# One Trainium2 core, attention and a state-space scan: statistics of seven batches, the last chunk's gates, the rooms of the end and two pools of PSUM banks are placed anew

## What is computed

```python
x1 = x * s1[:, None, :]
x1 = (x1 - mu) * rsqrt(var + 1e-5)                  # per token
q, k = heads(x1 @ Wq.T * q_dc), heads(x1 @ Wk.T * k_dc)      # 16 heads of 32
v = x1 @ Wv.T * v_dc * s2
x = x + (softmax(q k' / sqrt(32)) v) @ Ww.T * w_dc + v @ Wu.T * u_dc
xr, gate = split(x @ W_in.T)                         # 1024 each
xn = layernorm(silu(conv4(xr + cond))) * ln_g + ln_b
B, C, dt = split(xn @ W_xproj.T);  dt = tanh(dt @ W_dt.T + b_dt) * 0.01
h = clip(h * (1 - dt * tanh(A_log)) + B * min(|xn|, 1) * xn_t, -10, 10)   # 1024 steps
x = x + ((C . h + D * xn) * silu(gate)) @ W_out.T
```

## Time and profile before

| what | us |
|---|---|
| median of 3 timed runs (7177.43 to 7194.07) | 7184.33 |
| profiled execution | 7179.22 |
| its span | 7177.1 |

### The profile page before, as it was taken

The page is one execution under the profiler, slowest core; times in us unless marked ns, Lnnn a source line. Parts: engine busy times, 40 slices in busy tenths (PEclk is TensorE's granted clock), DMA queues, the critical chain, the costliest instruction groups (busy, mean ns, idle before and its releaser), DMA issues. The chain is left out here.

```text
span 7177.1 us, 72778 instructions
## 1 busy us (share of the span) xinstructions
PE 6304.4 (88%) x24000; PEld 2629.8 (37%) x24000; DVE 4763.7 (66%) x5810; ACT 2326.0 (32%) x4453; POOL 3308.7 (46%) x2631
## 2 busy tenths in 40 slices
PE   3899989999998999999865889999999989999897
PEld 1344434444343444444332223333333333333223
DVE  4554554555454555555426988889898889889890
ACT  1243343433444343343423223223232323223101
POOL 4366465665656574565714233324234343324312
PEclk7799999999999999999977779899998989899999
DMA  5221222222222222212123233434334333334432
GB/s 159 53 86 54 79 65 84 79 62 85 54 79 74 79 73 62 84 51 85 38 95 93 74 86 107 110 84 112 90 106 110 106 110 101 108 81 113 107 90 81
DMA packets 416040, 618.30 MB, mean 86 GB/s; under 512 B 59152, under 2 KB 192528, under 8 KB 415152
## 3 DMA queue, kind: packets, MB, share of 16 engines
q1 hardware_dynamic: 378800, 563.28, 27.8%
q10 hardware_dynamic: 36864, 50.38, 2.8%
HBM read 310.36 MB, written 201.38 MB: 71 GB/s over the span
## 5 line engine op out<-in xcount | busy, mean ns | idle before, releaser
L1018 POOL TENSOR_TENSOR acc<-acc,prob 128x512 f32<-128x512 f32 x1536 | 1903.2, 1280 | 1190.3 <-PE bank L737 954.7
L946 DVE TENSOR_REDUCE mx<-bank 128x1 f32<-128x512 f32 x2048 | 1322.3, 686 | 785.6 <-PE bank L707 783.9
L1710 DVE SCALAR_TENSOR_TENSOR g<-xps,bd,g 128x1024 f32<-128x1024 f32 x1024 | 1313.4, 1283 | 220.7 <-PE xps L1498 145.2
L707 PE MATMUL bank<-khat,qhat 96*128 96x512 f32 x2048 | 1010.2, 531 | 39.0 <-DMA khat<-halves 16.5
L1716 DVE TENSOR_SCALAR g<-g,lim 128x1024 f32<-128x1024 f32 x1024 | 1007.9, 984 | 28.6
L858 ACT ACTIVATE prob<-misc 128x512 f32<-128x512 f32 x1195 | 682.7, 601 | 567.9 <-PE misc L724 382.3
L1498 PE MATMUL xps<-sx,spread 16*128 16x512 f32 x2048 | 539.4, 529 | 279.3 <-DVE g L1710 263.0
L1861 POOL TENSOR_TENSOR y_t<-y_t,dx_t 128x512 f32<-128x512 f32 x120 | 172.4, 1457 | 1286.9 <-DMA y_t<-scratch_y 1286.9
L1513 PE MATMUL yps<-g,cexp 128*32 128x512 f32 x4096 | 709.3, 688 | 11.3 <-DVE g L1716 11.2
L724 PE MATMUL misc<-qhat,khat 98*128 98x512 f32 x1366 | 596.2, 464 | 131.2 <-ACT prob L858 104.6
L707 PEld LDWEIGHTS bank<-khat,qhat 96*128 96x128 f32 x2048 | 379.9, 194 | 546.6 <-issue 371.5
(11 more groups left out here) (183 smaller groups left out, 7038.8 us busy)
## 6 DMA issues: line engine op xcount, KB each, us to landing
sx<-scratch_xhl SPq DMA_DIRECT2D x512, 128.0 KB, 4.9
scratch_dx<-dx SPq DMA_DIRECT2D x64, 512.0 KB, 3.9
scratch_xhl<-xhi SPq DMA_DIRECT2D x64, 512.0 KB, 5.2
scratch_xhl<-xn SPq DMA_DIRECT2D x64, 512.0 KB, 5.5
scratch_y<-ysb SPq DMA_DIRECT2D x512, 64.0 KB
dx_t<-scratch_dx SPq DMA_DIRECT2D x60, 512.0 KB, 6.1
y_t<-scratch_y SPq DMA_DIRECT2D x60, 512.0 KB, 3.5
qhat<-halves SPq DMA_DIRECT2D x384, 64.0 KB, 2.0
```

What stands on the lines that cost most here:

```text
L707: pe.matmul(bank[m][:, 0:QC], self.qhat[0:96, s, h, qt * P:(qt + 1) * P], self.khat[0:96, s, h, c * QC:(c + 1) * QC], start=True, stop=Tru ...
L946: dve.tensor_reduce(self.mx2[:, j // self.NQ, c:c + 1], bank[m][:, 0:QC], AX.X, ALU.max).then_inc(sem[f"dve_m{m}"], 1)
L1018: pool.tensor_tensor(self.acc[:, a, h, :], self.acc[:, a, h, :], self.prob[:, (n % 2) * GH + h, :], ALU.add).then_inc(sem["pool_acc"], 1)
L1710: dve.scalar_tensor_tensor(self.g[:, t % 4, :], self.xps[t % 2][:, :], self.bd[:, i % 2, tl:tl + 1], self.g[:, (t - 1) % 4, :], ALU.mult, ...
```

## The change

It has five parts.

- **Statistics.** The set-up takes the statistics of batch 0 alone. Its x is loaded ahead of the last three weights into `x0`, a view of `aoT`, multiplied there on GpSimd, and normalised from there. The other batches get a lane `statistics(b)` in the unit before (fractions 0.2 to 1.6 of the batch before's first unit): loads, GpSimd products, VectorE's mean and variance, one Sqrt on ScalarE, the reciprocal. The normalisation loads and multiplies these tiles again, as before.
- **Order of the start.** TensorE begins the plan after the last demodulation sums are read, ScalarE after batch 0's statistics; only the copies (`lay`) and GpSimd still wait for the stored rows. The first batch's values come behind its projection. The ones in khat are written by GpSimd.
- **Maxima by blocks.** The 64 tiles go in four blocks of query half and key half; a tile waits for its two of the four laid halves. The lanes of `project` and `maxima` get other fractions.
- **Pools.** Scores may take banks 0 to 3, side work banks 2 to 5.
- **End.** The last chunk's gates (`gates`: `zm` on TensorE, `zo` on ScalarE) run beside the last chunk's steps and go into `xn` and `xc`; `finish` of the last chunk has no gates of its own and three rooms, whose buffers are others than before.

```diff
+def score_tile(j, TT, NQ):
+    blocks = sorted(((qc, kc) for qc in range(NQ) for kc in range(NQ)), key=lambda v: (max(2 * v[0], 2 * v[1] + 1), v))
+    each = GH * TT // NQ
+    qc, kc = blocks[j // each]
+    h, t = divmod(j % each, TT // NQ)
+    return h, qc * (TT // NQ) + t, qc, kc
...
 def attention_plan(plan, B, TT, NQ):
     plan.bank = {}
     order = Order(plan, 8, (0.2, 0.5))
-    EXP, SIDE = (0, 1, 2), (3, 4, 5)
+    EXP, SIDE = (0, 1, 2, 3), (2, 3, 4, 5)
     U, n_steps = B * GROUPS, NQ * TT
     def lane():
         out = []
         return out, lambda *a, **k: out.append(item(*a, **k))
+    def statistics(b):
+        out, put = lane()
+        put("SP", 0.6, ("sb_row", b), (("nb_mul", b - 1, TT - 1),) if b > 1 else (), [("ld_brow", 16)], lands=3.0)
+        for tt in range(TT):
+            s = tt % 2
+            old = ("sb_st", b, tt - 2) if tt > 1 else ("nb_nrm", b - 1, TT - 2 + tt)
+            put("SP", 0.6, ("sb_ld", b, tt), (old,) if b > 1 or tt > 1 else (), [(f"ld_xn{s}", 16)], lands=3.0)
+            put("POOL", 1.3, ("sb_mul", b, tt), (("sb_row", b), ("sb_ld", b, tt)), [("pool_n", 1)])
+            put("DVE", 0.7, ("sb_st", b, tt), (("sb_mul", b, tt),), [("dve_st", 1)])
+            put("DVE", 0.2, ("sb_ag", b, tt), (("sb_st", b, tt),), [("dve_st", 1)])
+        put("DVE", 0.2, ("sb_e", b), (("sb_ag", b, TT - 1),), [("dve_st", 1)])
+        put("ACT", 2.9, ("sb_sq", b), (("sb_e", b),), [("act_sq", 1)])
+        put("DVE", 0.3, ("sb_r", b), (("sb_sq", b),), [("dve_st", 2)])
+        return out
     def normalise_batch(b):
         out, put = lane()
-        put("SP", 0.6, ("nb_row", b), (("nb_mul", b - 1, TT - 1),) if b else (), [("ld_brow", 16)], lands=3.0)
         for tt in range(TT):
             s = tt % 2
-            old = ("nb_nrm", b, tt - 2) if tt > 1 else ("nb_nrm", b - 1, TT - 2 + tt)
-            put("SP", 0.6, ("nb_ld", b, tt), (old,) if b or tt > 1 else (), [(f"ld_xn{s}", 16)], lands=3.0)
-            put("POOL", 1.3, ("nb_mul", b, tt), (("nb_row", b), ("nb_ld", b, tt)), [("pool_n", 1)])
+            if b:
+                old = ("nb_nrm", b, tt - 2) if tt > 1 else ("sb_st", b, TT - 2 + tt)
+                put("SP", 0.6, ("nb_ld", b, tt), (old,), [(f"ld_xn{s}", 16)], lands=3.0)
+                put("POOL", 1.3, ("nb_mul", b, tt), (("nb_ld", b, tt),), [("pool_n", 1)])
             old = ("nb_tr", b, tt - 1) if tt else ("nb_tr", b - 1, TT - 1)
-            put("ACT", 0.6, ("nb_nrm", b, tt), (("nb_mul", b, tt),) + ((old,) if b or tt else ()), [("act_n", 1)])
+            put("ACT", 0.8, ("nb_nrm", b, tt), (("nb_mul", b, tt), ("sb_r", b)) * (b > 0) + ((old,) if b or tt else ()),
+                [("act_n", 1)])
             g = ("nb_tr", b, tt)
...
         out, put = lane()
-        put("SP", 0.6, ("mv_row", b), (("mv_o", b - 1, TT - 1),) if b else (), [("ld_vrow", 16)], lands=3.0)
+        put("SP", 0.6, ("mv_row", b), (("mv_o", b - 1, TT - 1),) if b else (("nb_ev", 0, TT - 1),),
+            [("ld_vrow", 16)], lands=3.0)
+        first = () if b else (("pm", 0, 2 * NQ - 1, HT - 1),)
         used = tuple(("C", b * GROUPS - 2 - k, n_steps - 1) for k in range(3)) if b else ()
         used += (("sk_tr", b - 1, TT - 1),) if b else ()
         for tt in range(TT):
             g = ("mv", b, tt)
...
             g = ("mx", u, j)
-            put("PE", 0.24, g, tuple(("cat", u, k, part) for k in range(2 * NQ) for part in range(2)),
+            _, _, qc, kc = score_tile(j, TT, NQ)
+            put("PE", 0.24, g, tuple(("cat", u, k, part) for k in (2 * qc, 2 * kc + 1) for part in range(2)),
                 [("pe_m{m}", 1)], take=SIDE, group=g)
             put("DVE", 0.69, ("mr", u, j), (g,), [("dve_m{m}", 1)], group=g, give=True)
...
         if u + 1 < U:
-            side(project(u + 1), -0.2, 0.05)
-            side(maxima(u + 1), 0.1, 0.85)
+            side(project(u + 1), -0.1, 0.15)
+            side(maxima(u + 1), 0.05, 0.85)
         if g == 0:
             side(finish_batch(b - 1), 0.1, 0.7) if b else side(scale_weights(0, 1), 0.1, 0.9)
+        if g == 0 and b + 1 < B:
+            side(statistics(b + 1), 0.2, 1.6)
         if g == 1:
             side(skip_path(b), -0.1, 0.9)
...
         c, n = divmod(k, 2)
         s, to = u % 2, (self.qhat, self.khat)[n]
+        w.wait_ge(sem["st_rows"], 16)
         w.wait_ge(sem["act_hi"], plan.after("act_hi", ("hi", u, k)))
         self.of_bank(w, "dve", ("pm", u, k), ("lo", u, k))
...
         tiles = lambda a: a.rearrange("(t p) o -> p t o", p=P)
         sp.dma_start(self.condT[:, :, :], d["condT"].rearrange("(t p) b -> p t b", p=P)).then_inc(sem["ld_cond"], 16)
+        for n, name in enumerate(("wqT", "wkT")):
+            sp.dma_start(self.wsq[:, n, :, :], tiles(d[name])).then_inc(sem[f"ld_w{n}"], 16)
+        sp.dma_start(self.brow[:, 0, :], d["cond"][0, 0:HID].partition_broadcast(P)).then_inc(sem["ld_s1"], 16)
+        for n in range(self.TT // 2):
+            sp.dma_start(self.x0[:, 2 * n:2 * n + 2, :], tiles(d["x"][0, 2 * n * P:2 * (n + 1) * P, :])).then_inc(
+                sem[f"ld_x0{n}"], 16)
+        for n, name in enumerate(("wvT", "wwT", "wuT")):
+            sp.dma_start(self.wsq[:, 2 + n, :, :], tiles(d[name])).then_inc(sem[f"ld_w{2 + n}"], 16)
         sp.dma_start(self.s2row[:, :], d["cond"][:, HID:2 * HID]).then_inc(sem["ld_s2"], 16)
-        for n, name in enumerate(("wqT", "wkT", "wvT", "wwT", "wuT")):
-            sp.dma_start(self.wsq[:, n, :, :], tiles(d[name])).then_inc(sem[f"ld_w{n}"], 16)
         sp.dma_start(self.wv[:, :, :], tiles(d["wvT"])).then_inc(sem["ld_wv"], 16)
-        for b in range(self.B):
-            w.wait_ge(sem["s_pool"], (b - 1) * self.TT)
-            sp.dma_start(self.s1b[:, b % 2, :], d["cond"][b, 0:HID].partition_broadcast(P)).then_inc(
-                sem[f"ld_s1{b % 2}"], 16)
-            for tt in range(self.TT):
-                i = b * self.TT + tt
-                w.wait_ge(sem["s_pool"], i - 3)
-                sp.dma_start(self.xin[:, i % 4, :], d["x"][b, tt * P:(tt + 1) * P, :]).then_inc(
-                    sem[f"ld_xs{i % 4}"], 16)
-        w.wait_ge(sem["s_dve"], 6)
-        sp.dma_start(d["rows"], self.rows[:, :, :]).then_inc(sem["st_rows"], 16)
     def sync(self, sp):
         d, sem, plan, w, TT, QC = self.d, self.sem, self.plan, Waits(sp), self.TT, self.QC
-        w.wait_ge(sem["st_rows"], 16)
-        w.wait_ge(sem["x_dve"], 2 * self.B * self.TT + 4)
-        w.wait_ge(sem["s_act"], 10)
-        w.wait_ge(sem["s_pe"], 4)
         tiles = lambda a: a.rearrange("(t p) o -> p t o", p=P)
...
         sem, plan, w, TT, QC = self.sem, self.plan, Waits(pe), self.TT, self.QC
         ident, bank = self.ident, self.bank
-        w.wait_ge(sem["st_rows"], 16)
-        w.wait_ge(sem["ld_wv"], 16)
-        w.wait_ge(sem["x_dve"], 2 * self.B * TT + 4)
...
         w.wait_ge(sem["ld_cond"], 16)
         act.activation(self.condT[:, :, :], self.condT[:, :, :], ACT.Square).then_inc(sem["s_act"], 1)
-        for n in range(5):
+        for n in range(2):
+            w.wait_ge(sem[f"ld_w{n}"], 16)
+            act.activation(self.wsq[:, n, :, :], self.wsq[:, n, :, :], ACT.Square).then_inc(sem["s_act"], 1)
+        w.wait_ge(sem["x_dve"], 2 * self.TT + 1)
+        act.activation(self.rstd[:, 0:self.TT], self.rstd[:, 0:self.TT], ACT.Sqrt).then_inc(sem["x_act"], 1)
+        for n in range(2, 5):
             w.wait_ge(sem[f"ld_w{n}"], 16)
             act.activation(self.wsq[:, n, :, :], self.wsq[:, n, :, :], ACT.Square).then_inc(sem["s_act"], 1)
...
+LAST_ROOMS = 3
+def room_before(i, b, room, NCH, B):
+    step = LAST_ROOMS if i == NCH - 1 else 1
+    if b >= step:
+        return i, b - step
+    return (i - 1, B - 1) if i and not room else None
...
+    def gates():
+        out = []
+        put = lambda *a, **k: out.append(item(*a, **k))
+        i = NCH - 1
+        for b in (*range(HB, B), *range(HB)):
+            if b == 0:
+                put("SP", 2.0, ("lz",), (("zm", B - 1, 1, HT - 1),), [("ld_x2T", 16 * HT)], lands=3.0)
+            free = ("pj", i, 1, HB - 1, 1) if b >= HB else ("slo", i, 1, b)
+            for half in range(2):
+                g = ("zm", b, half)
+                for it in range(HT):
+                    put("PE", 0.88, ("zm", b, half, it), (("lx", i, 1) if b >= HB else ("lz",),),
+                        [("pe_m{m}", 1)] if it == HT - 1 else [], take=SIDE if it == 0 else None, group=g)
+                put("ACT", 0.6, ("zo", b, half), (("zm", b, half, HT - 1), free), [("act_m{m}", 1)], group=g, give=True)
+        return out
...
             order.lane(finish(i - 1, SIDE, 0, range(B)), t + 1.0, t + TOK + 1.0)
-    order.lane(finish(NCH - 1, ALL, 0, range(0, HB)), last - 1.0, last - 1.0)
-    order.lane(finish(NCH - 1, ALL, 1, range(HB, B)), last - 1.0, last - 1.0)
+        if i == NCH - 1:
+            order.lane(gates(), t + 0.1 * TOK, t + 0.9 * TOK)
+    for room in range(LAST_ROOMS):
```

(9 more changed lines are left out.)

305 lines of the change are left out of this document (194 added, 111 removed).

## The result

The kernel after takes 6889.0 us (median of 4 runs, 6875.4 to 6890.9), the kernel before beside it 7189.2; the ratio is 0.958, 95% interval 0.956 to 0.960. The forecast was 6958 us, its range 6860 to 7062.

| stage | before | after | difference | forecast |
|---|---|---|---|---|
| to the first scores | 252.8 | 149.4 | -103 | -126 |
| attention | 3350.7 | 3192.2 | -159 | -50 |
| to the first scan step | 266.9 | 265.6 | -1 | 0 |
| scan steps | 3131.2 | 3169.0 | +38 | +30 |
| behind the last step | 175.5 | 112.0 | -64 | -80 |

A forecast was written before the change was run, and what follows sets the result against it. TensorE bounds attention (92% busy); VectorE and TensorE are both near full in the last chunk. Set-up -126, attention -50, last chunk +30, end -80 sum to -226: 7184.3 becomes 6958 us, range 6860 to 7062.

The forecast's parts named there:

- the value matmuls lie on TensorE beside this: Set-up: the first batch's value matmuls run beside the maxima, leaving VectorE the bound, 42 us to 121.
- 127 for the first scores: Set-up: attention's first scores come at 127 us instead of 252.8, a gain of 126 us.
- 70 us of waits before scores: Attention: of TensorE's 184 us of waits before score matmuls, 70 us are taken back.
- two of four copy laps: Attention: two of ScalarE's four copy laps already had projections beside them; part of the 70 us estimate.
- floor: Attention: at most 150 of TensorE's 271 idle us can be recovered, with the statistics hidden.
- Rival D: Attention gives 150 us since nearly all waits have one cause; total 6858 us, chance 0.09.
- B: Attention: shared banks cost more than they give, as side groups hold them; attention +60, total 7068 us, chance 0.14.
- The 20 us: Attention: seven batches' statistics cost ScalarE 7 x 2.9 = 20 us for table loads and roots.
- nothing for VectorE: Attention: the statistics' work on VectorE, about 8 us a batch, was charged at nothing.
- the 2.9 of the sum: Attention: one Sqrt between exponentials takes ScalarE 2.9 us, two table loads of 2.6 plus 0.3.
- the 24: End: sums and product, then first transpose and copy, are done 24 us after the last step.
- 2 for order: End: 2 us added for order to 93, making 95 us instead of 175.5.

The follow-up runs named there:

- e11: e5 with the first batch's values giving way to its maxima and chunk 6's finish due before the last step; 6803.4 us, ratio 0.946.
- e2: The kernel after with the old fractions of projection and maxima, and maxima tiles waiting for all four laid halves; 7144.2 us, ratio 0.993.
- e3: The kernel after with both the old maxima order and fractions and the old separate PSUM bank pools; 7131.3 us, ratio 0.992.
- e5: The kernel after with the statistics' two small VectorE operations (adding epsilon, minus mean times root) made by GpSimd; 6841.2 us, ratio 0.951.
- e8: The kernel before with only the maxima by blocks and the new fractions of projection and maxima; 7031.6 us, ratio 0.977.
- e9: e5 with the old fractions of projection and maxima, the blocks kept; 7088.7 us, ratio 0.986.
- e10: e5 with maxima tiles waiting for all four laid halves again, the new fractions kept; 6948.9 us, ratio 0.966.
- e1: The kernel after with separate PSUM bank pools again (scores 0 to 2, side work 3 to 5); 6928.1 us, ratio 0.962.
- e7: The kernel after with the Sqrt of batches 1 to 7 replaced by a copy, so no table switch in attention; 6879.6 us, ratio 0.956.
- e6: e3 with the statistics' two small VectorE operations made by GpSimd, as in e5; 7051.6 us, ratio 0.980.

## Why the prediction was right in sum, and which of its terms were wrong

The spans differ by 289 us where the sum had 226. That the total lies in the range is in part luck: attention gave 109 us more than its term, the set-up 23 and the end 16 less, and the other scan steps 8 less.

- **Set-up, -103 instead of -126.** Up to the first high half every time is right to 1 us. The step that failed is "the value matmuls lie on TensorE beside this": the items of the start have one due time, and the planner put the values first, 27.63 us in a block. e11 shows both sides: without that the maxima run from 79.8 to 120, as forecast (79 and 121), but 127 for the first scores needed nearly all the values beside the maxima. In e11 only 16 of 64 value matmuls stand ahead of the dense block of maxima, the rest behind it.
- **Attention, -159 instead of -50.** This is the term that was mis-sized, by 109 us, in three places. First, I took back 70 us of waits before scores; 108 went (184 to 76). I had taken two of four copy laps as covered; that this is why the 70 was too low is argued, no run shows it. Second, I counted idle time alone. Where TensorE idles less, the granted clock mostly stands higher (324 and 344 us idle at 0.95 and 0.94 in e2 and e3, 271 at 0.96 in before, 147 at 0.97 in after, 132 at 0.98 in e5; but e8 has 0.98 with 186), and the same matmuls took 35 us less in after, 65 in e8. So the "floor" of -150 was none: e5 stands at -197. It isn't a law of these runs: busy time times clock is 2956 us in before and 2954 in after, each known to 15 us because the clock is read to 0.01, but 2991 and 3010 in e9 and e10, so there something else lengthens the matmuls. Third, the parts: the maxima edit is -150 alone (e8), the statistics are +42, and the shared banks -42 by the profiled executions (57 of e1 less 15 by which VectorE's two operations were longer there) or -17 by the medians (32 less 15). These sum to between -150 and -125 of the -159; 9 to 34 us stay unassigned. Rival D, at 0.09, had this size. What B describes fits the losses with the old fractions (e2, e9); with the new ones the sharing gained.
- **The statistics, +42 instead of +20, and for another reason.** The 20 us were charged to ScalarE's table loads. e7 takes the switches away and attention stays; "nothing for VectorE" was the failed step. 39 of the 42 us come from two operations that take 0.17 us each in the set-up and wait for GpSimd in attention (e5). In the old order one wait is up to 9.89 us, and both together cost 83 us by the medians and 118 by the profiled executions (e6). The Trainium skill's 5.3 us for a pair of switches (page "ScalarE: Activation LUTs", section "Table sets: the hidden batching unit") would have given 39 us, near the measured sum by chance. The trace doesn't agree with that figure: a pair with its root takes 2.84 us in e5, as the 2.9 of the sum had it, and attention doesn't pay it (e7). That ScalarE, busy 44% of attention, has room for it is my reading; no run tries it with ScalarE full.
- **Last chunk, +30: right** (312.5 to 342.8; the prediction's base of 307 was a stretch with 126 of the 128 steps, its difference holds). TensorE is busy 331.5 of 342.8 us, at a mean clock of 0.95; without gates 289.3 of 316.2, at 0.90. So the clock rose with the gates, as supposed; how many us that gave back wasn't measured. The other 8 us of the steps are within what the same scan varies.
- **End, -64 instead of -80.** GpSimd starts 9.8 us and the first transpose comes 19.7 us behind the last step at 6776.2 (forecast 11 and 21; the 24 counts its copy too). The "2 for order" was the mis-sized term. The last output matmuls of chunk 6 are due behind the last step, and the planner leaves four instructions of that group until nothing else is left, with the group's bank held from 6767.7 to 6856. The first room's copy waits 9.00 us for them, and its last batch starts late:

```profile
6786.01 2.48 POOL L2009 TENSOR_TENSOR y_t<-y_t,dx_t 128x512 f32<-128x512 f32 x2 [26.55 <-DMA y_t<-scratch_y]
...
6795.87 1.11 PE L1668 MATMUL yps<-ident,y_t 128*128 128x128 f32 x4 [18.53 <-POOL y_t L2022]
...
6854.10 1.88 PE L1675 MATMUL miscb<-w_out,ygT 128*128 128x512 f32 x4
...
6856.08 0.60 ACT L1818 ACTIVATE ygT<-yps 128x512 f32<-128x512 f32 x1 [9.00 <-PE miscb L1675]
...
6870.15 2.49 POOL L2009 TENSOR_TENSOR y_t<-y_t,dx_t 128x512 f32<-128x512 f32 x2 [40.71 <-DMA y_t<-scratch_y]
```

With their due time mended (e11) the end takes 88.0 us.
